# Attention and mixture of experts on one core: softmax sums inverted in two parts, row statistics by two tiles

## The chip, the core and the metric

The kernel runs on one NeuronCore of a Trainium2 chip. Engines are TensorE (PE in the profile, its weight loads PEld), VectorE (DVE), ScalarE (ACT), GpSimd (POOL) and SyncE (SP). Each works through its own queue in order, and they meet in semaphores. The metric is the device time of one execution in microseconds; lower is better.

## The reference, cut to what matters

For 2048 tokens of width 256, with 16 heads:

```python
x = x + layernorm(attention(layernorm(x)))      # causal, latent keys and values of width 64
x = x + layernorm(ffn(layernorm(x)))            # shared expert + 2 of 16 experts per token

scores = einsum('bhqd,bhkd->bhqk', qs, ks_) * scale
attn = softmax(where(causal, scores, min), axis=-1)
out = einsum('bhqk,bhkd->bhqd', attn, v) @ wo
router_logits = x @ gate_w
_, selected = top_k(sigmoid(router_logits) + expert_bias, 2)
```

## The kernel before, in words

The 2048 queries are four blocks of 512 (`qc` 0 to 3), each of four tiles of 128 rows (`TC`). In a block the 16 heads are taken as eight pairs (`p` 0 to 7), and each pair goes over the block's key tiles: 4, 8, 12 or 16 of them, as the attention is causal. One key tile of a pair is three slots, so a pair has 12, 24, 36 or 48 slots.

In a slot, hand-written order: TensorE makes the scores of the pair (`scores`, L1699, with `kt` the key tile and `s` the head), ScalarE the exponentials into a ring of four tiles of probabilities (`scores_to_probs`, L759), GpSimd adds the probabilities up (`add_up`, L560 and L567), TensorE multiplies them by the values (`values`, L1720) into PSUM bank `BK_O`. Before its exponentials, a score bank is seeded with minus the row maximum by ScalarE (`seed`, through the `copy` of L646). The maxima are those of the next pair, made in the same slots one pair ahead: TensorE makes rough scores (`max_unit`, L1673) into banks 4 and 5, VectorE takes their maxima (`maxima`, L1124, L1126), then per head TensorE spreads the maxima over columns (`spread`, L1681) into bank `BK_M` and VectorE copies them out (`widen`, L1142). `units_by` says how many of these units are due at a slot. VectorE also folds each pair's added probabilities into `Lp` (`part_sums`, L1182). Blocks 1 and 2 project the next block's queries in their slots, and block 3 casts the experts' weights (`cut_expert`).

At the end of a block come, by TensorE's order: primes and filler matmuls (`stay_busy`, L1662, which write zeros into a bank that is free), the sums of all 16 heads from `Lp` (L1844), ten fillers, the turning of the inverse sums (L1852), three fillers. VectorE takes the reciprocal (L1360) and splits it into three 16-bit terms (`terms`, L1211 to L1215), ScalarE copies the turned terms out as `inv_rows`. TensorE spreads a pair's inverse sums over its rows (`inv_spread`, L1823), VectorE multiplies the pair's values by them (`normalised`, L1223), and TensorE multiplies by the output weights (`out_product(j, n)`, tile `j`, pair `n`, L1832). Each tile then has its statistics on VectorE, a root on ScalarE, the input added, statistics and root again, and scaled rows (`out_moments`, `with_input`, `row_moments`, `row_scale`, and on ScalarE `root` and `normalised_rows`). VectorE's `choose` and `places` pick the experts of the block before. The next block's first scores wait for the third tile's rows, its first exponential stands on ScalarE behind the fourth tile's last root:

```python
for j in range(TC):
    root(qc, j, 0)
    if 0 < j < TC - 1:
        normalised_rows(qc, j - 1)
    if j < TC - 1:
        root(qc, j, 1)
    if j == TC - 2 and qc < NC - 1:
        act.wait_ge(primed, 2 * (qc + 1) + 2)
        seed(qc + 1, 0, 1)
```

After block 3, the rows are transposed (`turn_xn2`, L1607), routed, and the experts run on gathered rows.

Of the kernel before, what the change touches and what calls it, by code (L numbers as in the profile page):

```python
# [58 lines left out]
ROOTS = 2 + (NT - TC) // 2  # L59

# [15 lines left out]
def attention_moe(nc, x, wq, wkv_a, wkv_b, wo, kv_scale, gate_w, bias, sh_gate, sh_up, sh_down,  # L76
                  ex_gu, ex_down, c32_d, c16_d, out):
    with ExitStack() as ctx:  # L78
# [116 lines left out]
        mask_row = c32[:, C_COS + 2 * CQ:C_COS + 2 * CQ + CQ // 2].bitcast(BF16)  # L195

# [42 lines left out]
        den_read, log_out = sem("den_read"), sem("log_out")  # L239
# [32 lines left out]
        def units_by(slot, qc, p):  # L272

            nq = qc + (p == NP - 1)
            U, slots = units(nq), 3 * tiles_of(qc)
            if Q_IN_LOOP(qc) and p % 2 and nq == qc:

                return min(U, sum(TURN_UNITS[:slot]) + max(slot - len(TURN_UNITS), 0))
            return min(U, slot + min(slot, max(U - slots, 0)))

        def spread_slots(qc, p):
# [5 lines left out]
            second = units(nq) + (4 if Q_IN_LOOP(qc) and p % 2 else 2)  # L287
            return first, min(second, 3 * tiles_of(qc))
# [35 lines left out]
        def inv_bank(n):  # L324

            return BK_O if n % 2 else BK_M

        def first_root(qc, j):

            return ROOTS + 2 * (qc * TC + j)  # L330

# [300 lines left out]
        def _(act):  # L632
# [111 lines left out]
            def scores_to_probs(qc, p):  # L744
# [4 lines left out]
                for kt in range(KT):  # L749
# [42 lines left out]
            def root(qc, j, r):  # L792

                act.wait_ge(var_ready, first_root(qc, j) + r + 1)
                nc.scalar.activation(std[:, TC * r + j:TC * r + j + 1], var[:, TC * r + j:TC * r + j + 1],
                                     ACT.Sqrt).then_inc(std_ready, 1)

            def normalised_rows(qc, j):

                y, x1 = (ysb3, x13) if qc == NC - 1 else (yb, xb)  # L800
                act.wait_ge(scale_ready, qc * TC + j + 1)
# [29 lines left out]
            for qc in range(NC):  # L831
                if qc == NC - 1:
                    act.wait_ge(shared_in, 80)
                    copy(WEh[:, NE, :], stage[:, 0, :], WS).then_inc(raw_hi, 1)
# [4 lines left out]
                if qc:  # L839
                    root(qc - 1, TC - 1, 1)  # L840
# [8 lines left out]

                if qc < NC - 1:  # L850
                    act.wait_ge(primed, 2 * (qc + 1) + 1)
                    seed(qc + 1, 0, 0)

                act.wait_ge(turned_ready, qc + 1)
                copy(inv_rows[0:3 * H, :], ps[0:3 * H, BK_O, :]).then_inc(inv_ready, 1)
                if qc < NC - 1:
                    act.wait_ge(rows_out, 32 * qc)
                for j in range(TC):
# [1157 lines left out]
```

## Time and profile before

| | |
|---|---|
| median of 3 runs | 1311.3 us (1304.27 to 1312.95) |
| the profiled execution | 1306.9 us |
| its span, first to last instruction | 1305.1 us |
| mean granted TensorE clock | 0.968 |
| TensorE busy | 1154.6 us (88%) |
| VectorE busy | 832.9 us (64%) |
| ScalarE busy | 795.2 us (61%) |
| GpSimd busy | 732.5 us (56%) |

In a timeline a row gives the start, the busy time, the engine, the line, what is written and read, and the number of instructions put together; in brackets stands the idle time of the engine before it and what ended that. Times are microseconds from the span's start. A matmul's printed time includes its way through the array, so starts follow one another more closely than these times say.

### The profile page before, as it was taken

What the parts mean: (1) busy time and instruction counts of PE and PEld (TensorE: products, weight loads), DVE (VectorE), ACT (ScalarE), POOL (GpSimd) and SP (SyncE); (2) the same over time, 40 slices, a digit from 0 to 9 for tenths busy, and PEclk for the clock granted to TensorE, in tenths of its full rate; (3) what the DMA queues carried; (4) which work ended last, traced back from release to release, by engine and by line L of the source; (5) the groups of instructions that cost most, each with busy time, mean ns of one, the idle gap of its engine ahead of it and who ended that gap; (6) DMA issues with size and microseconds to landing.
All of it is one profiled execution on the core that took longest, in us unless ns stands there. A gap on an engine that the chain in (4) does not pass through costs nothing. (4 is left out here: it accounts for less than half of the span.)

```text
span 1305.1 us, 19781 instructions
## 1 busy us (share of the span) xinstructions
PE 1154.6 (88%) x6552; PEld 549.4 (42%) x6563; DVE 832.9 (64%) x2104; ACT 795.2 (61%) x1237; POOL 732.5 (56%) x444
## 2 busy tenths in 40 slices
PE   3997999999998999999999979999999999788820
PEld 2643545344443533444443523333433334466710
DVE  6556786666667766565756786676666625745637
ACT  3633762766665466766666367777787783356632
POOL 0046541465564076766666248888888894435545
PEclk9988999999999999999999999999999999989975
DMA  9135300110011010000011001000000000367754
GB/s 286 34 87 131 91 1 1 49 33 17 21 45 34 6 44 17 17 17 17 17 33 32 11 13 57 26 13 13 25 25 25 13 13 17 71 130 211 187 135 141
DMA packets 63031, 70.25 MB, mean 54 GB/s; under 512 B 10080, under 2 KB 52448, under 8 KB 62816
## 3 DMA queue, kind: packets, MB, share of 16 engines
q1 hardware_dynamic: 56656, 56.26, 15.8%
q0 software_dynamic: 4864, 10.51, 3.7%
q10 hardware_dynamic: 1424, 2.38, 0.7%
q8 instruction: 48, 0.79, 0.3%
q14 instruction: 39, 0.32, 0.1%
HBM read 37.51 MB, written 14.83 MB: 40 GB/s over the span
## 5 line engine op out<-in xcount | busy, mean ns | idle before, releaser
L567 POOL TENSOR_TENSOR D<-D,B 128x1024 f32<-128x1024 f32 (+3 forms) x256 | 513.4, 2006 | 140.5 <-ACT B L759 120.2
L759 ACT ACTIVATE B<-ps 128x1024 f32<-128x1024 f32 (+1 forms) x320 | 285.2, 892 | 206.6 <-PE ps L1699 121.0
L1124 DVE TENSOR_REDUCE mxp<-ps 128x1 f32<-128x512 f32 x384 | 260.4, 688 | 177.2 <-PE ps L1673 175.1
L646 ACT ACTIVATE ps<-D 128x1024 f32<-128x1024 f32 (+3 forms) x327 | 288.3, 883 | 24.1 <-DVE D L1142 14.4
L1720 PE MATMUL ps<-B,kv 128*64 128x512 f32 (+3 forms) x1280 | 278.9, 545 | 0.3
L1699 PE MATMUL ps<-A,KTh 128*128 128x512 f16 (+3 forms) x768 | 209.0, 354 | 4.0 <-ACT ps L646 3.9
L560 POOL TENSOR_TENSOR D<-B 128x1024 f32<-128x1024 f32 (+1 forms) x32 | 70.8, 2213 | 209.1 <-ACT B L759 209.1
L1126 DVE CUSTOM_DVE_ANT_0 ps<-ps,c 128x128 f32<-128x128 f32 (+3 forms) x256 | 126.6, 496 | 76.9 <-PE ps L1673 73.4
L1673 PE MATMUL ps<-KTh,A 128*128 128x512 f16 (+3 forms) x384 | 134.4, 357 | 10.4 <-DVE mxp L1124 8.7
L1699 PE MATMUL ps<-A,KTl 128*128 128x512 f16 (+3 forms) x384 | 135.8, 354 | 0.0
L1720 PEld LDWEIGHTS ps<-B,kv 128*64 128x64 f32 x1280 | 73.6, 135 | 113.7 <-issue 97.0
L1699 PEld LDWEIGHTS ps<-A,KTh 128*128 128x128 f16 x768 | 67.6, 98 | 82.0 <-issue 21.4
L1673 PEld LDWEIGHTS ps<-KTh,A 128*128 128x128 f16 x384 | 37.0, 97 | 113.3 <-DVE mxp L1124 45.4
L646 ACT ACTIVATE C<-ps 128x256 f16<-128x256 f32 (+2 forms) x112 | 52.5, 470 | 50.5 <-PE ps L1893 15.5
L586 POOL DMA_INDIRECT B<-xn_rows,tok_i x48 | 45.4, 946 | 50.1 <-PE ps L1893 49.2
L1699 PE MATMUL ps<-WEh,KTh 128*128 128x512 f16 (+3 forms) x256 | 67.1, 345 | 2.5 <-ACT ps L646 2.3
L1832 PE MATMUL ps<-WO,C 128*128 128x256 f32 x256 | 64.7, 393 | 3.1 <-DVE C L1223 3.1
L1699 PE MATMUL ps<-WEl,KTh 128*128 128x512 f16 (+3 forms) x256 | 65.8, 340 | 0.6 <-ACT ps L646 0.6
L1541 PE MATMUL ps<-xnTh,WQh 128*128 128x512 f16 (+1 forms) x160 | 55.5, 347 | 4.5 <-DVE WEl L1260 1.8
L646 ACT ACTIVATE B<-ps 128x256 f32<-128x256 f32 (+2 forms) x132 | 44.0, 336 | 21.9 <-PE ps L1852 17.0
L1701 PE MATMUL ps<-c 128*128 128x128 bf16 x256 | 56.3, 220 | 0.0
L1543 PE MATMUL ps<-xnTh,WQl 128*128 128x512 f16 (+1 forms) x160 | 55.3, 346 | 0.0
(273 smaller groups left out, 1785.3 us busy)
## 6 DMA issues: line engine op xcount, KB each, us to landing
results<-B SPq DMA_DIRECT2D x64, 128.0 KB
xnTl<-in_L_ffn_experts_gate_up SPq DMA_DIRECT2D x16, 256.0 KB, 2.8
A<-in_L_attn_wq SPq DMA_DIRECT2D x4, 768.0 KB, 20.6
B<-in_L_attn_x SPq DMA_DIRECT2D x5, 512.0 KB, 5.6
D<-in_L_attn_wo SPq DMA_DIRECT2D x2, 1024.0 KB, 20.3
A<-C SPq DMA_DIRECT2D x16, 128.0 KB, 2.3
A<-C SPq DMA_DIRECT2D x32, 64.0 KB, 2.0
A<-stg SPq DMA_DIRECT2D x16, 128.0 KB, 2.3
```

The lines of the kernel that those rows point to most:

```text
L560: ins = nc.gpsimd.tensor_tensor(acc[:, :, c0:], Pr[:, 0, :, c0:], Pr[:, 1, :, c0:], ALU.add)
L567: nc.gpsimd.tensor_tensor(acc[:, :, c0:], acc[:, :, c0:], Pr[:, kt % P_RING, :, c0:], ALU.add).then_inc(sum_done, 1)
L646: return nc.scalar.activation(dst, src, ACT.Copy, scale=scale)
L759: nc.scalar.activation(Pr[:, kt % P_RING, :, c0:], ps[:, 2 * (kt % ST_RING):2 * (kt % ST_RING) + 2, c0:], ACT.Exp, scale=SM_SCALE).then_in ...
L1124: V.tensor_reduce(most, rough, AX.X, ALU.max).then_inc(mx_free, 1)
L1126: V.tensor_tensor_reduce(rough, rough, mask_qk(w), 1.0, 2 * NEG, ALU.add, ALU.max, most).then_inc(mx_free, 1)
L1541: T.matmul(dst, ah, bh, start=first, stop=False)
L1673: T.matmul(ps[:, b, 0:w], qt(qc, 2 * p + s, 0)[:, i4 * P:(i4 + 1) * P], KTh[:, kc * CQ:kc * CQ + w], start=True, stop=True).then_inc(mx_re ...
L1699: ins = T.matmul(ps[:, bk, c0:], k[:, keys], v, start=False, stop=True, skip_group_check=True)
L1701: ins = T.matmul(ps[:, bk, c0:c0 + P], identb, mask_kq, start=False, stop=True, skip_group_check=True)
L1720: ins = T.matmul(ps[LORA * s:LORA * (s + 1), BK_O, c0:], kv[:, kt, 0:LORA], Pr[:, kt % P_RING, s, c0:], start=(kt == 0), stop=(kt == KT - 1))
L1832: ins = T.matmul(ps[:, y_bank(j), 0:E], OT[:, o:o + P], WO[:, n, :], start=(n == 0), stop=(n == NP - 1))
```

## The change

The inverse sums of pairs 0 to 5 are made inside pair 7: TensorE makes the sums at one slot and turns the terms at a later one, given for each block in `EARLY`, VectorE makes the reciprocal and its terms in the slot after the first, ScalarE copies the turned terms out. At the block's end only pairs 6 and 7 (`LATE_PAIRS`) are left for the old way, and the fillers there are four instead of 18 (after block 3, 29). The output products of tiles 0 and 1 start at once on pairs 0 to 5. VectorE and ScalarE handle the row statistics of two tiles at a time. The next block's first scores wait for the second tile's rows instead of the third's; the maxima made in pair 0 start four slots later (`HEAD_SLOTS`), and the cast of the shared expert's weights moves from the start of block 3 into its pair 0.

```diff
+EARLY = [(3, 6), (18, 21), (24, 28), (6, 10)]
+LATE_PAIRS = 2
+HEAD_SLOTS = 4
...
+            if qc and p == 0:
+
+                return min(U, max(slot - HEAD_SLOTS, 0))
...
         def inv_bank(n):
 
-            return BK_O if n % 2 else BK_M
+            return 2 + n % 2
...
+                    if qc == NC - 1 and p == 0 and kt == 3:
+                        act.wait_ge(shared_in, 80)
+                        copy(WEh[:, NE, :], stage[:, 0, :], WS).then_inc(raw_hi, 1)
...
+                    if p == NP - 1 and kt == EARLY[qc][1] // 3:
+                        act.wait_ge(e_turned_ready, qc + 1)
+                        copy(early_rows[0:3 * H, :], ps[0:3 * H, BK_M, :]).then_inc(e_inv_ready, 1)
...
-                for j in range(TC):
-                    root(qc, j, 0)
-                    if 0 < j < TC - 1:
-                        normalised_rows(qc, j - 1)
...
+                roots_of(qc, 0, 0)
+                roots_of(qc, 0, 1)
+                roots_of(qc, 2, 0)
+                normalised_rows(qc, 0)
                 if qc < NC - 1:
-                    act.wait_ge(rows_out, 32 * qc)
...
+                    act.wait_ge(primed, 2 * (qc + 1) + 2)
+                    seed(qc + 1, 0, 1)
+                normalised_rows(qc, 1)
+                roots_of(qc, 2, 1)
...
+                    if p == NP - 1 and slot == EARLY[qc][0] + 1:
+                        dve.wait_ge(e_den_ready, qc + 1)
+                        link(V.reciprocal(rL[:, :, :].rearrange("p h j -> p (h j)"), ps[:, BK_M, 0:H * TC]))
+                        terms(early_terms, early_rest, e_terms_ready)
...
+                for n in range(2):
+                    normalised(qc, n)
                 part_sums(qc, NP - 1)
+                for n in range(2, NP - LATE_PAIRS):
+                    normalised(qc, n)
...
+                out_moments(qc, 0)
+                if qc:
+                    places(qc - 1, 1, 3)
+                with_input(qc, 0)
+                row_moments(qc, 0)
+                out_moments(qc, 2)
+                row_scale(qc, 0)
+                with_input(qc, 2)
+                row_moments(qc, 2)
+                row_scale(qc, 2)
...
+                    if p == NP - 1 and slot == EARLY[qc][0]:
+
+                        pe.wait_ge(l_done, CR_L + qc * NP + NP - LATE_PAIRS)
+                        pe.wait_ge(wide_done, 2 * (nq * NP + np_) + int(Q_IN_LOOP(qc)))
+                        sums_of_parts(BK_M, e_den_ready)
+                    if p == NP - 1 and slot == EARLY[qc][1]:
+                        pe.wait_ge(e_terms_ready, qc + 1)
+                        turn_terms(early_terms, BK_M, e_turned_ready)
...
-                stay_busy(5 if qc < NC - 1 else 16)
...
-                stay_busy(10)
...
-                stay_busy(3)
...
+                stay_busy(4, 1)
+                for n in range(NP - LATE_PAIRS):
+                    for j in range(2):
+                        out_product(j, n)
+                    if n + 2 < NP - LATE_PAIRS:
+                        inv_spread(n + 2)
+                    if n == 2:
+
+                        pe.wait_ge(l_done, CR_L + (qc + 1) * NP)
+                        sums_of_parts(0, den_ready)
...
+                pe.wait_ge(terms_ready, qc + 1)
+                turn_terms(inv_terms, 1, turned_ready)
...
+                for j in range(3):
+                    for n in range(NP - LATE_PAIRS, NP):
+                        out_product(j, n)
...
+                for n in range(NP):
+                    out_product(3, n)
                 if qc < NC - 1:
-                    pe.wait_ge(z_ready, qc * TC + 3)
...
+                    pe.wait_ge(z_ready, qc * TC + 2)
```

TensorE in pair 7 of block 1, from slot 18 on, first the order of before, then that of the changed kernel. `KTh` with `WEh` is a unit of the next block's maxima, `KTh`, `KTl` with `A` are scores, `B` with `kv` values, and `Lp` the sums.

```order
L1673 MATMUL ps<-KTh,WEh 128x512
L1699 MATMUL ps<-A,KTh 128x256 x2
L1699 MATMUL ps<-A,KTl 128x256
L1701 MATMUL ps<-c 128x128
L1673 MATMUL ps<-KTh,WEh 128x512
L1720 MATMUL ps<-B,kv 64x512 x2
L1673 MATMUL ps<-KTh,WEh 128x384
L1699 MATMUL ps<-A,KTh 128x128 x2
L1699 MATMUL ps<-A,KTl 128x128
L1701 MATMUL ps<-c 128x128
L1673 MATMUL ps<-KTh,WEh 128x512
```

```order
L1757 MATMUL ps<-Lp,c 32x64 x4
L1702 MATMUL ps<-KTh,WEh 128x512
L1728 MATMUL ps<-A,KTh 128x256 x2
L1728 MATMUL ps<-A,KTl 128x256
L1730 MATMUL ps<-c 128x128
L1702 MATMUL ps<-KTh,WEh 128x512
L1749 MATMUL ps<-B,kv 64x512 x2
L1702 MATMUL ps<-KTh,WEh 128x384
L1728 MATMUL ps<-A,KTh 128x128 x2
L1728 MATMUL ps<-A,KTl 128x128
L1730 MATMUL ps<-c 128x128
L1764 MATMUL ps<-c,scr_r 48x128 x4
```

The sums (L1757) now stand ahead of slot 18's unit, and the turning of the terms (L1764) between the scores of the last key tile's first head and slot 21's unit. VectorE at the same place, before and changed:

```order
L1124 TENSOR_REDUCE mxp<-ps 128x1 x2
L1126 ISA ps,mxp<-ps,c 128x384
L1126 ISA mxp 128x1
L1124 TENSOR_REDUCE mxp<-ps 128x1 x2
L1126 ISA ps,mxp<-ps,c 128x512
```

```order
L1138 TENSOR_REDUCE mxp<-ps 128x1 x2
L1178 RECIPROCAL rL<-ps 128x64
L1233 CAST scr_r<-rL 128x16x4
L1234 TENSOR_TENSOR scr_r<-rL,scr_r 128x64
L1236 CAST scr_r<-scr_r 128x16x4
L1237 TENSOR_TENSOR scr_r<-scr_r 128x16x4
L1140 ISA ps,mxp<-ps,c 128x384
L1140 ISA mxp 128x1
L1138 TENSOR_REDUCE mxp<-ps 128x1 x2
```

The reciprocal and its four terms stand between the units of slots 19 and 20. TensorE at the end of block 1, from the last values product, before and changed; `c` alone is a prime, a filler or (64x512) a spread of inverse sums, `WO,C` an output product:

```order
L1720 MATMUL ps<-B,kv 64x128 x2
L1656 MATMUL ps<-c 128x512 x2
L1662 MATMUL ps<-c 128x512 x5
L1844 MATMUL ps<-Lp,c 32x64 x4
L1662 MATMUL ps<-c 128x512 x10
L1852 MATMUL ps<-c,B 48x128 x4
L1662 MATMUL ps<-c 128x512 x3
L1823 MATMUL ps<-B,c 64x512 x4
L1832 MATMUL ps<-WO,C 128x256
L1823 MATMUL ps<-B,c 64x512 x2
L1832 MATMUL ps<-WO,C 128x256
```

```order
L1749 MATMUL ps<-B,kv 64x128 x2
L1882 MATMUL ps<-c 64x512 x4
L1691 MATMUL ps<-c 128x512 x4
L1891 MATMUL ps<-WO,C 128x256 x2
L1882 MATMUL ps<-c 64x512 x2
L1891 MATMUL ps<-WO,C 128x256 x2
L1882 MATMUL ps<-c 64x512 x2
L1891 MATMUL ps<-WO,C 128x256 x2
L1882 MATMUL ps<-c 64x512 x2
L1757 MATMUL ps<-Lp,c 32x64 x4
L1891 MATMUL ps<-WO,C 128x256 x2
L1882 MATMUL ps<-c 64x512 x2
```

The output products now follow the last values product after two spreads and four fillers, two tiles per pair, and the sums of the late pairs stand behind the third pair's products.

## Rows read from the trace of the kernel before

**Rows 1.** Stretches: start:end, length, busy time (instructions) of PE, PEld, DVE, ACT, POOL; clock, DMA.
```profile
234.40:402.00 167.60, 163.13 (x954) 69.89 (x954) 111.48 (x263) 110.49 (x141) 94.91 (x50) 1.00 0.13 32
...
757.10:760.30 3.20, 3.13 (x9) 1.21 (x10) 1.66 (x5) 2.65 (x4) 0.00 (x0) 0.51 0.38 123
```

**Rows 2.** Timeline of TensorE from the end of block 1 into block 2.
```profile
421.70 0.38 PE L1656 MATMUL ps<-c 128*128 128x512 bf16 x1 [0.16 <-issue]
...
423.49 2.33 PE L1662 MATMUL ps<-c 128*128 128x512 bf16 x10
...
428.74 0.40 PE L1823 MATMUL ps<-B,c 48*64 48x512 bf16 x2
...
439.30 7.07 PE L1832 MATMUL ps<-WO,C 128*128 128x256 f32 x32
446.21 0.59 PE L1699 MATMUL ps<-WEh,KTh 128*128 128x512 f16 x2
...
453.56 0.60 PE L1699 MATMUL ps<-WEh,KTh 128*128 128x512 f16 x2 [0.98 <-ACT ps L646]
```

**Rows 3.** Timeline of ScalarE from the end of block 1 into block 2.
```profile
449.17 0.20 ACT L795 ACTIVATE std<-var 128x1 f32<-128x1 f32 x1 [1.69 <-DVE var L974]
...
450.68 1.02 ACT L759 ACTIVATE B<-ps 128x1024 f32<-128x1024 f32 x1
451.60 0.59 ACT L802 ACTIVATE WEh<-WEl,shiftb,rstd 128x256 f32<-128x256 f32 x1
...
452.49 1.01 ACT L646 ACTIVATE ps<-D 128x1024 f32<-128x1024 f32 x1
```

**Rows 4.** Timeline of TensorE after block 3, the row transposes.
```profile
1118.58 1.09 PE L1607 MATMUL ps<-c,B 128*128 128x128 f32 x8 [0.59 <-ACT B L804]
```

**Rows 5.** Timeline of VectorE at the end of block 1.
```profile
423.69 0.56 DVE L1360 RECIPROCAL rL<-ps 128x64 f32<-128x64 f32 x1 [0.61 <-PE ps L1844]
424.28 0.31 DVE L1211 CAST B<-rL 128x64 bf16<-128x64 f32 x1
...
425.28 0.44 DVE L1215 TENSOR_TENSOR B<-B 128x64 bf16<-128x64 f32 x1
...
439.52 0.42 DVE L1228 BATCH_NORM_STATS2 st<-ps 128x6 f32<-128x256 f32 x1
```

**Rows 6.** Timelines of TensorE and VectorE in pair 7 of blocks 0 to 3.
```profile
195.75 0.39 PE L1673 MATMUL ps<-KTh,A 128*128 128x512 f16 x1
...
417.05 0.38 PE L1673 MATMUL ps<-KTh,WEh 128*128 128x512 f16 x1
...
719.37 1.29 DVE L1124 TENSOR_REDUCE mxp<-ps 128x1 f32<-128x512 f32 x2 [0.23 <-PE ps L1673]
...
720.83 0.38 PE L1673 MATMUL ps<-KTh,A 128*128 128x512 f16 x1
...
1057.14 1.94 PE L1720 MATMUL ps<-B,kv 128*64 128x512 f32 x8
```

**Rows 7.** Timeline of GpSimd in pair 7 of blocks 1, 2 and 3.
```profile
412.33 6.59 POOL L567 TENSOR_TENSOR D<-D,B 128x1024 f32<-128x1024 f32 x4 [3.06 <-ACT B L759]
...
720.25 4.32 POOL L567 TENSOR_TENSOR D<-D,B 128x1024 f32<-128x1024 f32 x2 [1.11 <-ACT B L759]
...
1057.28 32.68 POOL L567 TENSOR_TENSOR D<-D,B 128x1024 f32<-128x1024 f32 x14
```

**Rows 8.** Timelines of GpSimd and VectorE; two VectorE lines, ns min/median/max.
```profile
767.13 2.35 POOL L567 TENSOR_TENSOR D<-D,B 128x1024 f32<-128x1024 f32 x1 [0.51 <-ACT B L759]
...
767.25 2.25 DVE L1331 CAST where_i<-where 128x8 uint32<-128x8 f32 x1
...
L1302 DVE TENSOR_TENSOR share<-share,rsum x4: 166/168/2091, 467.5 to 1187.2; 128x8 f32<-128x8 f32 x4
...
L1321 DVE COPY scr_r<-place x4: 182/183/187, 457.4 to 1127.8; 128x64 f32<-128x64 f32 x4
```

**Rows 9.** Timeline of TensorE in the first pair of block 3.
```profile
757.17 0.61 PE L1673 MATMUL ps<-KTh,A 128*128 128x512 f16 x1 [2.82 <-DVE mxp L1124]
```

More of the change, by code:

```diff
@@ L287, in spread_slots @@
             second = units(nq) + (4 if Q_IN_LOOP(qc) and p % 2 else 2)
+            if qc and p == 0:
+                first, second = first + HEAD_SLOTS, second + HEAD_SLOTS
             return first, min(second, 3 * tiles_of(qc))
@@ new lines, in row_moments, with row_scale @@
+            def row_moments(qc, j0):
+                x1 = x13 if qc == NC - 1 else xb
+                for j in (j0, j0 + 1):
+                    dve.wait_ge(z_ready, qc * TC + j + 1)
+                    ins = V.bn_stats(st6[:, TC + j, :], x1[:, j, :])
+                link(ins)
+                for j in (j0, j0 + 1):
+                    ins = V.bn_aggr(mv[:, TC + j, :], st6[:, TC + j, :])
+                link(ins)
+                variance(TC + j0 + 2, LN_EPS, first=TC + j0)
+            def row_scale(qc, j0):
+                two = slice(TC + j0, TC + j0 + 2)
+                one_over(TC + j0 + 2, first=TC + j0)
+                V.scalar_tensor_tensor(out=shiftb[:, two], in0=mv[:, two, 0], scalar=-1.0, in1=rstd[:, two],
@@ L1722, in values, with sums_of_parts, turn_terms @@
                 ins.then_inc(pv_done, 1)
+            def sums_of_parts(bank, ready):
+                parts = Lp[:, :, :].rearrange("p h (j b) -> p h j b", b=4)
+                for b in range(4):
+                    ins = T.matmul(ps[32 * b:32 * b + 32, bank, 0:H * TC], quads, parts[:, :, :, b],
+                                   start=True, stop=True)
+                ins.then_inc(ready, 1)
+            def turn_terms(terms, bank, ready):
+                for j in range(TC):
+                    ins = T.matmul(ps[0:3 * H, bank, j * P:(j + 1) * P],
+                                   terms[:, j, :, :].rearrange("p w h -> p (w h)"), identb,
+                                   start=True, stop=True)
+                ins.then_inc(ready, 1)
             def pair(qc, p):
@@ L1817, in inv_spread @@
                 def inv_spread(n):
+                    rows = early_rows if n < NP - LATE_PAIRS else inv_rows
                     if n >= 2:
@@ L1847, in _ @@
-                pe.wait_ge(o_free, CR_O + (qc + 1) * NP)
-                stay_busy(10)
-                pe.wait_ge(terms_ready, qc + 1)
-                for j in range(TC):
-                    ins = T.matmul(ps[0:3 * H, BK_O, j * P:(j + 1) * P],
-                                   inv_terms[:, j, :, :].rearrange("p w h -> p (w h)"), identb,
-                                   start=True, stop=True)
-                ins.then_inc(turned_ready, 1)
-                stay_busy(3)
-                pe.wait_ge(inv_ready, qc + 1)
```

171 lines of the change are left out of this document (76 added, 95 removed).

## The prediction

> **What bounds the kernel now.** I read the stretches first. Inside the attention blocks TensorE is the pace: it is busy 163.1 of 167.6 us at the full clock in block 1 [rows 1]. Between the blocks it isn't. TensorE's timeline of the end of block 1 [rows 2] shows 24.5 us from the last values product (421.70) to the next block's first scores (446.21), of which 18 filler matmuls (5, 10 and 3 by the code; the ten take 2.33) do nothing, and the inverse sums go through VectorE, TensorE and ScalarE before the first output product can start. ScalarE's timeline [rows 3] shows what comes last there: the root of the fourth tile's second variance (449.17), the table load behind it, and only then the next block's first exponential (450.68), 29.0 us after 421.70. TensorE takes up scores again 2.9 us after that exponential (453.56), once the next seed is in. The same distance is 28.8 and 28.9 us after blocks 0 and 2; block 3 has no next block and ends in the row transposes at 1118.58 [rows 4]. So the change has to be judged by three things: what it puts into the full last pairs, how much earlier the next exponential comes, and how much earlier the transposes come.
>
> **Term A, the early sums inside the last pair.** Each block's pair 7 gets four more sums matmuls and four turning matmuls on TensorE (about 0.35 us each group, 0.7 together), one copy of 0.6 us on ScalarE, and on VectorE a reciprocal, two casts and two subtractions, which took 2.03 us in a row from 423.69 to 425.72 [rows 5]. TensorE now waits in its own queue for those terms before it turns them, so scores, maxima and values behind it stand. What counts is when VectorE gets to the reciprocal and when the terms are done.
>
> Where TensorE comes to the turning is read from the matmul that follows it now [rows 6]: 195.75 in block 0, 417.05 in block 1, 720.83 in block 2, 1057.14 in block 3. VectorE has to do the maximum ahead of the reciprocal first. In block 2 that is the first of the two from 719.37 [rows 6], which the sums put off by 0.35, so it ends at 720.4; by the same reading it ends at 195.6 and 416.7 in blocks 0 and 1. In block 3 it has no maxima, so the sums, done at about 1054.8, start it. With 2.0 us for the terms and 0.35 for turning, the matmul behind comes 2.3, 2.1 and 2.1 us late in blocks 0 to 2 (198.1, 419.2, 722.9), and not late in block 3, where the terms would be done at 1056.9. Nothing gives that back: TensorE has no idle time behind it in block 2, and in blocks 0 and 1 its one wait there is for VectorE's maxima, which come later by the same step.
>
> But GpSimd adds up probabilities just then [rows 7], and small VectorE operations between SBUF tiles are held by it: the cast of 0.17 us took 2.25 us from 767.25 and ended with the GpSimd addition that had begun at 767.13, and a subtraction-like operation of 0.17 us took 2.09 [rows 8]. I take the two subtractions as held and the two casts as free, because these casts (0.31 us, 16-bit results written with a stride) don't run at the speed of the plain copy of as many elements (0.18 us) [rows 5, 8]. Block 0: an addition ends at 197.4, the next needs an exponential that TensorE now keeps back; terms at 198.5, turned at 198.85, 3.1 us late. Block 1: the third of the four additions ends at about 418.35 (the sums themselves shift it by 0.35); terms at 419.45, 2.8 late. Block 2: two additions follow each other, ending at 722.6 and 724.5; the first subtraction waits for one, the second for the other; terms at 725.0, 4.6 late. Block 3: additions end at 1057.14 and 1059.7, terms at 1060.15, turned at 1060.5. There GpSimd is what bounds the pair, 14 additions without a pause to 1089.96 [rows 7]; its fifth addition comes 2.9 us later than now (values 1.9, scores 1.3, exponential 1.0 behind 1060.5, against 1057.28 and two additions of 2.33, 1061.95). Sum of A: 3.1 + 2.8 + 4.6 + 2.9 = 13.4. Bounds: all terms free, 2.3 + 2.1 + 2.1 + 0 = 6.5; casts held too, one more addition in blocks 2 and 3, 3.6 + 3.0 + 5.2 + 5.5 = 17.3.
>
> The Trainium skill's page SBUF — State Buffer, section Who interferes with whom, says that a VectorE instruction with two SBUF inputs, or a copy or cast in a two-port mode, and a GpSimd instruction shut each other out for the whole instruction. The held rows agree with it. By it alone the casts would be held where they run in that mode, which makes A 17.3 and is the slower rival below; if it did not bite here, A would be 6.5.
>
> **Term B, the stretch between blocks.** Worked out on block 1. TensorE from 421.70: two spread pairs (0.33 us each), four fillers (0.9); then per pair two output products (0.87, as 32 passes take 7.07) and a spread, 1.2 us against VectorE's 0.7, so TensorE no longer waits for VectorE; sums, turning, primes. Together 64 passes 14.1 + eight spreads 2.7 + 0.9 + 0.75 + 0.9 = 19.3: it is through at 441.0, 5.2 earlier. VectorE's terms (done 431.2) and ScalarE's copy lie beside products of tiles 0 to 2.
> The next exponential gains less. Tiles 0 and 1 are complete at 436.2; two statistics (0.42 each, [rows 5]), aggregates and variance to 437.2; table load and root to 438.75; scale and two multiply-adds to 439.95; second statistics to 441.25. Tiles 2 and 3 follow: variance 442.45, multiply-adds 443.9, second variance 445.25. ScalarE in the meantime does row pair 0, seed and row pair 1 (0.89, 1.0 and 0.89 by [rows 3]) from 442.8 to 445.6; root to exponential takes 1.51, so the exponential is at 447.1 instead of 450.68: 3.6 earlier. This takes the place of the single-tile chain; last is now ScalarE's row pair 1, 0.3 behind VectorE. Three blocks: 10.8.
> Block 3: the last part sum needs GpSimd's end at 1090; the sixth pair's products end at 1096.5, terms 1097.6 and VectorE's choice of experts to 1099.3, late pairs' products to 1103.0, tile 3 to 1106.7. Then second variance 1110.75 and two row pairs to 1113.3, against 1118.5: 5.2 earlier, and all that follows moves with it. B = -(10.8 + 5.2) = -16.0. Bounds: TensorE's own gain between the blocks, -(3 x 5.2 + 5.2) = -20.8; each ScalarE and VectorE operation at its full printed time instead of the distance of starts, -(3 x 2.7 + 4.0) = -12.1.
>
> **Terms C and D.** C: the maxima of pair 0 start four slots later. TensorE has then done two instead of six of them when it takes up scores again, 0.86 us of work moved into a full stretch, less its waits for VectorE there (up to 1.0 a block); 0.4 per block, 1.2, bounds 0 and 2.6. The shared weights' cast (0.83 us ScalarE, 0.95 VectorE) moves off the start of block 3, but that start waits for the root chain anyway: nothing; it would cost its own 0.95 once if VectorE's maxima in pair 0 waited on it.
> D: the clock. TensorE stood idle for 2.82 us before 757.17 [rows 9], and the 3.2 us from 757.10 ran at a granted clock of 0.51, the 1.2 GHz level [rows 1]; the wait of 0.98 before 453.56 was followed by full-speed matmuls [rows 2]. One such loss is 1.5 us. In the changed kernel TensorE has nothing from about 446.6 to 449.95 (3.4 us) after block 1, and as much after block 0; block 3's start had its loss already. The stop in block 2's last pair is 3.8 us. So three losses, 4.5; bounds 0 and five (with block 3's stop and the wait before the transposes), 7.5.
>
> **Sum.** 13.4 - 16.0 + 1.2 + 4.5 = +3.1. The profiled execution took 1306.9 us (span 1305.1), 4.4 below the median of 1311.3 of the runs shown, so 1310.0 beside it and 1314.4, rounded 1314, beside the median. About 1% (13 us) is what a measurement of this kernel can tell from no change.
>
> **Rivals.** First, faster: VectorE's early terms meet GpSimd idle or aren't held, and the stop in block 2 costs no clock. Then 6.5 - 16.0 + 1.2 + 3.0 = -5.3, 1306. For it: every row of the same five operations ran free [rows 5]; against: those ran while GpSimd was idle. Second, faster by more: TensorE's own 5.2 us decide between the blocks, not the exponential, and no clock is lost: 6.5 - 20.8 + 0 + 0 = -14.3, 1297. Against it stands the 2.9 us between exponential and scores, which only ScalarE sets. Third, slower: GpSimd holds all four early operations, and each long stop loses the clock: 17.3 - 16.0 + 1.2 + 7.5 = +10.0, 1321; in block 3, at half clock, values and scores behind the stop take 3.2 us more and GpSimd's row of additions ends later by as much, 1324.5. It decides from the point where terms take longer than 4 us instead of 2.0; the held cast speaks for it [rows 8]. Fourth, the change doesn't do what it says: the exponential waits as now for the last tile's root, the three 3.6 us are not gained: +13.9, 1325.
>
> **Chances and range.** Forecast 0.43, first rival 0.27, second 0.12, third 0.14, fourth 0.04. The range 1300 to 1324 leaves out the second rival and the upper half of the third and fourth, about 0.2. Faster by over 1% (below 1298): the second rival and a bit, 0.13; slower by over 1% (above 1324): 0.13; within 1%: 0.74.
>
> **What would show it.** Term A: in the last pairs VectorE's four early operations should take over 1 us more than 1.5 in blocks 2 and 3, with TensorE idle for 2 to 5 us ahead of its turning matmuls. If these are free everywhere, A is wrong and the time is at most 1306. Term B: first exponential 25.4 us after the last values product instead of 29.0, transposes 23.3 us after GpSimd's last addition instead of 28.6. Term D: granted clock near 0.5 for some 3 us at the start of blocks 1 and 2. A time outside 1300 to 1324 would make the whole wrong.

## The result and the profile after

| | before | changed |
|---|---|---|
| median of the runs | 1309.37 us (4 runs, 1304.27 to 1312.95) | 1324.06 us (4 runs, 1321.1 to 1325.84) |
| ratio to before | | 1.0113, 95% interval 1.0071 to 1.0154 |
| profiled execution, span | 1305.1 us | 1323.0 us |

The change makes the kernel 14.7 us slower where 3.1 more were forecast; 1324.06 lies just outside the range of 1300 to 1324.

Where the 17.9 us between the two profiles lie is read best from ScalarE's exponentials, 320 in both, always in the same order. Each stretch runs between the starts of two of them: of a last pair from its first to its last, of a first pair, and of pairs 1 to 6, from its first to the first of the pair behind. The last column is the prediction's terms, put at the stretch they were meant for.

| stretch, by ScalarE's exponentials | before | changed | difference | predicted |
|---|---|---|---|---|
| start of the program to pair 1 of block 0 | 139.83 | 141.26 | +1.4 | 0 |
| block 0, pairs 1 to 6 | 50.94 | 50.94 | 0 | 0 |
| block 0, pair 7, first to last | 8.06 | 14.10 | +6.0 | 3.1 |
| last of block 0 to first of block 1 | 32.69 | 29.26 | -3.4 | -3.6 |
| block 1, pair 0 | 20.96 | 22.81 | +1.9 | 0.4 + 1.5 |
| block 1, pairs 1 to 6 | 141.28 | 141.28 | 0 | 0 |
| block 1, pair 7 | 23.93 | 26.64 | +2.7 | 2.8 |
| last of block 1 to first of block 2 | 32.99 | 29.35 | -3.6 | -3.6 |
| block 2, pair 0 | 33.51 | 35.74 | +2.2 | 0.4 + 1.5 |
| block 2, pairs 1 to 6 | 206.60 | 206.61 | 0 | 0 |
| block 2, pair 7 | 34.29 | 42.22 | +7.9 | 4.6 + 1.5 |
| last of block 2 to first of block 3 | 31.84 | 28.47 | -3.4 | -3.6 |
| block 3, pair 0 | 46.62 | 51.83 | +5.2 | 0.4 |
| block 3, pairs 1 to 6 | 248.06 | 248.05 | 0 | 0 |
| block 3, pair 7, to GpSimd's last addition | 38.37 | 45.21 | +6.8 | 2.9 |
| from there to the row transposes | 28.61 | 23.37 | -5.2 | -5.2 |
| behind the row transposes | 186.53 | 185.82 | -0.7 | 0 |

Between the blocks the prediction holds within 0.3 us everywhere. The last pairs cost 23.5 us instead of 14.9, the first pairs of blocks 1 to 3 cost 9.3 instead of 4.2. These are the two errors, 8.6 and 5.1 us.

**The gain between the blocks, as forecast.** TensorE's timeline of the changed kernel from the end of block 1 into block 2, which answers to [rows 2]:

```profile
429.84 0.62 PE L1882 MATMUL ps<-c 48*64 48x512 bf16 x4
...
437.08 2.86 PE L1891 MATMUL ps<-WO,C 128*128 128x256 f32 x12
...
449.75 0.59 PE L1728 MATMUL ps<-WEh,KTh 128*128 128x512 f16 x2
...
454.78 0.59 PE L1702 MATMUL ps<-KTh,WEh 128*128 128x512 f16 x2
458.51 1.04 PE L1728 MATMUL ps<-WEh,KTh 128*128 128x512 f16 x2 [3.14 <-ACT ps L661]
```

ScalarE's timeline of the same place, which answers to [rows 3]:

```profile
446.06 1.28 ACT L817 ACT_TABLE_LOAD   x1 [2.56 <-DVE var L988]
...
453.25 0.58 ACT L823 ACTIVATE WEh<-WEl,shiftb,rstd 128x256 f32<-128x256 f32 x1
...
455.63 1.02 ACT L774 ACTIVATE B<-ps 128x1024 f32<-128x1024 f32 x1
```

Products start as soon as the last values product is through (429.84), scores of block 2 are issued 19.9 us behind it instead of 24.5, and the first exponential stands 25.8 us behind it (455.63) instead of 29.0. Then TensorE has nothing to do for 3.14 us: the stop is nearly as long as the prediction had it (3.4). The row transposes come 23.4 us behind the end of GpSimd's last addition (1113.77), against 28.6 [rows 4, 7]. GpSimd's and TensorE's timelines:

```profile
1086.09 27.68 POOL L582 TENSOR_TENSOR D<-D,B 128x1024 f32<-128x1024 f32 x12 [7.01 <-ACT B L774]
...
1137.14 1.40 PE L1636 MATMUL ps<-c,B 128*128 128x128 f32 x8 [2.38 <-ACT B L825]
```

**The stops in the last pairs.** VectorE's timeline of the early sums in block 2, where [rows 5] has the same five operations with GpSimd idle:

```profile
727.64 0.55 DVE L1178 RECIPROCAL rL<-ps 128x64 f32<-128x64 f32 x1
728.22 2.20 DVE L1233 CAST scr_r<-rL 128x64 bf16<-128x64 f32 x1
730.46 1.86 DVE L1234 TENSOR_TENSOR scr_r<-rL,scr_r 128x64 f32<-128x64 f32 x1
732.36 0.31 DVE L1236 CAST scr_r<-scr_r 128x64 bf16<-128x64 f32 x1
732.70 0.44 DVE L1237 TENSOR_TENSOR scr_r<-scr_r 128x64 bf16<-128x64 f32 x1
```

GpSimd's timeline there: two additions, from 727.91 to 732.20.

```profile
727.91 4.29 POOL L582 TENSOR_TENSOR D<-D,B 128x1024 f32<-128x1024 f32 x2 [1.55 <-ACT B L774]
```

The cast of 0.31 us took 2.20: it waited for the first of the two additions, the subtraction behind it for the second, and ended 0.12 us after it (732.32 against 732.20). The groups of these operations by line, over all four blocks (busy us, mean ns of one). The reciprocal, which reads PSUM, has its usual length, and the last subtraction, which met no addition in any block, has its own:

```profile
L1233 DVE CAST scr_r<-rL 128x64 bf16<-128x64 f32 x4 | 5.8, 1456 | 0.1
L1234 DVE TENSOR_TENSOR scr_r<-rL,scr_r 128x64 f32<-128x64 f32 x4 | 4.9, 1216 | 0.1
L1236 DVE CAST scr_r<-scr_r 128x64 bf16<-128x64 f32 x4 | 3.4, 856 | 0.1
...
L1178 DVE RECIPROCAL rL<-ps 128x64 f32<-128x64 f32 x4 | 2.2, 551 | 8.2 <-PE ps L1757 8.2
...
L1237 DVE TENSOR_TENSOR scr_r<-scr_r 128x64 bf16<-128x64 f32 x4 | 1.8, 445 | 0.1
```

TensorE's stops at the turning, in blocks 0 to 3:

```profile
200.28 0.62 PE L1764 MATMUL ps<-c,scr_r 128*48 128x128 bf16 x4 [2.87 <-DVE scr_r L1237]
...
425.30 0.40 PE L1764 MATMUL ps<-c,scr_r 128*48 128x128 bf16 x4 [1.74 <-DVE scr_r L1237]
...
733.20 0.62 PE L1764 MATMUL ps<-c,scr_r 128*48 128x128 bf16 x4 [4.54 <-DVE scr_r L1237]
...
1079.78 0.51 PE L1764 MATMUL ps<-c,scr_r 128*48 128x128 bf16 x3 [5.61 <-DVE scr_r L1237]
```

Three of the four turnings take 0.5 or 0.6 us instead of 0.40: behind these stops the clock is down. The stretches (columns as in [rows 1]; the clock is the third figure from the end) show block 1 at full clock and then the slow ones: behind the stops of blocks 0, 2 and 3, at the start of block 2, and two in the first pair of block 3:

```profile
238.40:418.00 179.60, 172.97 (x1004) 74.27 (x1005) 121.63 (x286) 115.76 (x147) 99.65 (x52) 1.00 0.13 32
200.20:206.20 6.00, 5.92 (x29) 2.87 (x29) 2.72 (x10) 1.07 (x2) 1.27 (x1) 0.52 0.00 1
458.50:461.90 3.40, 3.39 (x9) 1.30 (x10) 2.47 (x4) 3.40 (x6) 1.84 (x1) 0.50 0.26 58
733.20:738.70 5.50, 5.50 (x18) 1.72 (x19) 1.74 (x5) 0.59 (x1) 0.00 (x0) 0.53 0.00 0
772.50:775.90 3.40, 3.35 (x10) 0.85 (x9) 3.20 (x7) 3.37 (x5) 2.98 (x2) 0.51 0.00 0
787.00:793.10 6.10, 6.03 (x14) 1.61 (x15) 3.53 (x9) 0.00 (x0) 1.61 (x1) 0.51 0.18 64
1079.80:1083.40 3.60, 3.60 (x12) 1.39 (x12) 0.00 (x0) 0.59 (x1) 0.00 (x0) 0.53 0.00 0
```

The stop at the start of block 1 is about as long as that of block 2 (3.14), and the clock stays up behind it:

```profile
238.44 0.60 PE L1728 MATMUL ps<-A,KTh 128*128 128x512 f16 x2 [3.30 <-ACT ps L661]
```

**The shared cast in the first pair of block 3.** VectorE's timeline of the kernel before, then VectorE's, GpSimd's and TensorE's of the changed kernel:

```profile
755.29 0.95 DVE L1347 SCALAR_TENSOR_TENSOR WEl<-xnTl,WEh 128x768 f16<-128x768 f32 x1
```

```profile
783.48 2.93 DVE L1195 SCALAR_TENSOR_TENSOR WEl<-xnTl,WEh 128x768 f16<-128x768 f32 x1
```

```profile
783.25 2.34 POOL L582 TENSOR_TENSOR D<-D,B 128x1024 f32<-128x1024 f32 x1 [2.85 <-ACT B L774]
785.75 2.86 POOL L582 TENSOR_TENSOR D<-D,B 128x1024 f32<-128x1024 f32 x1 [0.15 <-ACT B L774]
```

```profile
787.07 0.61 PE L1702 MATMUL ps<-KTh,A 128*128 128x512 f16 x1 [2.46 <-DVE mxp L1138]
787.61 3.68 PE L1749 MATMUL ps<-B,kv 128*64 128x512 f32 x8
```

The cast had taken 0.95 us at the start of block 3. Moved between GpSimd's additions it takes 2.93, the maxima behind it come late, TensorE stops for 2.46 us, and the eight values products behind the stop take 3.68 us instead of 1.94.

### The profile page after: what moved, and what is told of

Read it like the earlier page. It is cut to its first block and busy times, and to the rows that moved or that the text cites. A ratio compares the mean times of both kernels' runs of the same rounds, so it can differ in the third digit from the quotient of the medians.

```text
span 1323.0 us, 19712 instructions
## 1 busy us (share of the span) xinstructions
PE 1147.7 (87%) x6533; PEld 547.6 (41%) x6544; DVE 841.4 (64%) x2077; ACT 793.6 (60%) x1225; POOL 736.2 (56%) x444
## 5 line engine op out<-in xcount | busy, mean ns | idle before, releaser
L1749 PE MATMUL ps<-B,kv 128*64 128x512 f32 (+3 forms) x1280 | 285.0, 554 | 0.3
L589 POOL TENSOR_TENSOR B<-B 128x512 f32<-128x512 f32 x5 | 6.3, 1265 | 88.2 <-DVE B L1105 88.2
```

What stands on the lines that cost most here:

```text
L1749: ins = T.matmul(ps[LORA * s:LORA * (s + 1), BK_O, c0:], kv[:, kt, 0:LORA], Pr[:, kt % P_RING, s, c0:], start=(kt == 0), stop=(kt == KT - 1))
```

## The experiments

The theory after this reading: GpSimd's additions hold every VectorE operation that works from SBUF to SBUF, casts too; TensorE stops for them in the last pairs and in block 3's first pair, and its clock falls behind the stops. The rivals: TensorE's own place in its queue (too few slots between sums and turning), and the later start of the first maxima.

The ratios below are to runs of the kernel before that were taken beside each group of versions, with a median of 1313.07 us for the first five and of 1309.96 us for the four that put things together; so versions are compared by ratio and not by time. Fillers and the two profiles taken once more are single runs (1327.46, 1319.45 and 1329.11 us), read by their stretches alone.

The growth of each stretch against the kernel before, in us, from one profile of each version (first pairs of blocks 1 to 3; last pairs of blocks 0 to 3, the last to GpSimd's last addition; the three stretches between blocks; from GpSimd's last addition to the transposes):

| version | first pairs | last pairs | between blocks | to transposes |
|---|---|---|---|---|
| the change | 1.9, 2.2, 5.2 | 6.0, 2.7, 7.9, 6.8 | -3.4, -3.6, -3.4 | -5.2 |
| the change, second profile | 1.9, 2.2, 5.3 | 5.0, 2.7, 8.1, 6.9 | -3.4, -3.6, -3.4 | -5.2 |
| shared cast back | 3.5, 2.2, 1.3 | 3.4, 2.7, 8.1, 7.2 | -3.3, -3.6, -3.4 | -5.2 |
| terms through PSUM | 3.5, 2.2, 2.4 | 2.9, 2.5, 2.4, 0.0 | -3.3, -3.7, -3.4 | -3.8 |
| wide gap | 1.9, 3.5, 5.1 | 6.3, 3.0, 1.6, 0.0 | -3.4, -3.3, -2.4 | -2.1 |
| maxima from slot 0 | 0.0, 0.0, 3.3 | 6.2, 2.7, 8.0, 7.8 | -3.4, +0.5, -3.4 | -5.2 |
| fillers in block 3's stop | 3.5, 2.2, 5.4 | 3.4, 2.7, 8.1, 5.2 | -3.3, -3.7, -3.4 | -5.3 |
| PSUM, cast back | 3.5, 2.2, 1.1 | 2.9, 2.5, 2.4, 0.0 | -3.3, -3.6, -3.4 | -3.7 |
| PSUM, cast back, wide gap, maxima from slot 0 | 0.0, 0.0, 0.4 | 4.3, 2.5, 1.8, 0.0 | -3.4, -3.3, -2.4 | -3.8 |
| PSUM, cast back, maxima from slot 0 | 0.0, 0.0, 0.4 | 4.4, 2.5, 2.4, 0.0 | -3.3, -3.6, -3.4 | -5.2 |

**Shared cast back.** ScalarE's part between two roots of block 2's tail, VectorE's part ahead of block 3's first maxima:

```diff
-                    if qc == NC - 1 and p == 0 and kt == 3:
-                        act.wait_ge(shared_in, 80)
-                        copy(WEh[:, NE, :], stage[:, 0, :], WS).then_inc(raw_hi, 1)
...
                 roots_of(qc, 0, 0)
+                if qc == NC - 2:
+                    act.wait_ge(shared_in, 80)
+                    copy(WEh[:, NE, :], stage[:, 0, :], WS).then_inc(raw_hi, 1)
                 roots_of(qc, 0, 1)
...
-                    if qc == NC - 1 and p == 0 and slot == 13:
-                        dve.wait_ge(raw_hi, 1)
...
             for qc in range(NC):
+                if qc == NC - 1:
+                    dve.wait_ge(raw_hi, 1)
...
                 for p in range(NP):
```

> The shared expert's cast goes back out of block 3's first pair: ScalarE's part between the two roots of block 2's tail, VectorE's part ahead of block 3's first maxima, where GpSimd has nothing to do. Theory: in the first pair of block 3 the VectorE part was held by GpSimd's additions (2.93 us instead of 0.95), the maxima behind it came late, TensorE stopped for 2.46 us and then ran at half clock. Then the growth of that pair (5.2 us against the kernel before) falls below 1.5 and the whole comes to about 1319.5 us. Rival: the four slots by which the maxima start later are the cause; then the growth stays at 4 to 5 us and the time at 1324.

Measured: 1322.22 us, ratio 1.0079 (1.0049 to 1.011). The first pair of block 3 grows by 1.3 us instead of 5.2. VectorE's part, with GpSimd idle:

```profile
771.42 0.95 DVE L1373 SCALAR_TENSOR_TENSOR WEl<-xnTl,WEh 128x768 f16<-128x768 f32 x1
```

The theory holds for this pair: 4.0 us are the held cast, its stop and its clock; 1.3 are left, of which the later maxima are a part. Of the whole time the intervals of the two versions overlap, so the 4 us are shown by the profile alone.

**Terms through PSUM.** The reciprocal writes into free columns of the bank it reads, the remainder stays there too; nothing else moves:

```diff
-link(V.reciprocal(rL[:, :, :].rearrange("p h j -> p (h j)"), ps[:, BK_M, 0:H * TC]))
-terms(early_terms, early_rest, e_terms_ready)
+link(V.reciprocal(ps[:, BK_M, H * TC:2 * H * TC], ps[:, BK_M, 0:H * TC]))
+terms(early_terms, ps[:, BK_M, 2 * H * TC:3 * H * TC].rearrange("p (h j) -> p h j", h=H),
+      e_terms_ready, ps[:, BK_M, H * TC:2 * H * TC].rearrange("p (h j) -> p h j", h=H))
...
```

> The early reciprocal and the remainder are kept in PSUM, so each of VectorE's early casts and subtractions reads at least one operand from PSUM; count and order of the instructions stay. Theory: GpSimd's additions hold VectorE only where all its operands are in SBUF. Then the four operations take 1.5 to 2 us in every last pair (in the changed kernel 2.1, 1.9, 4.9 and 7.2), the growth of the four last pairs (6.0, 2.7, 7.9 and 7.5, together 24.2 us) falls to some 8 to 10, and the time is about 1309. Rival: they are slow because of the 16-bit results written with a stride into SBUF beside GpSimd's own writes; then they stay as long and the time stays at 1324.

Measured: 1313.7 us, ratio 1.0014 (0.9988 to 1.004). The groups by line, to be laid beside those of the change:

```profile
L1234 DVE CAST scr_r<-ps 128x64 bf16<-128x64 f32 x4 | 1.8, 445 | 0.1
L1237 DVE CAST scr_r<-ps 128x64 bf16<-128x64 f32 x4 | 1.8, 444 | 0.1
L1238 DVE TENSOR_TENSOR scr_r<-ps,scr_r 128x64 bf16<-128x64 f32 x4 | 1.8, 443 | 0.1
L1235 DVE TENSOR_TENSOR ps<-ps,scr_r 128x64 f32<-128x64 f32 x4 | 1.1, 268 | 0.1
```

In block 3, VectorE and GpSimd now run side by side:

```profile
1061.36 0.45 DVE L1234 CAST scr_r<-ps 128x64 bf16<-128x64 f32 x1
1061.84 0.27 DVE L1235 TENSOR_TENSOR ps<-ps,scr_r 128x64 f32<-128x64 f32 x1
1062.15 0.45 DVE L1237 CAST scr_r<-ps 128x64 bf16<-128x64 f32 x1
1062.63 0.45 DVE L1238 TENSOR_TENSOR scr_r<-ps,scr_r 128x64 bf16<-128x64 f32 x1
```

```profile
1060.59 2.35 POOL L575 TENSOR_TENSOR D<-B 128x1024 f32<-128x1024 f32 x1 [0.49 <-ACT B L774]
```

This is the decisive run. Same operations, same slots, same 16-bit results with a stride; what changed is that each reads one operand from PSUM (and the remainder is written there). None of the sixteen is held: the casts take 0.44 to 0.45 us in every block, the subtractions 0.27 and 0.44 as they do with GpSimd idle. The last pairs of blocks 2 and 3 lose 5.5 and 6.8 us of their growth and the kernel some 13 of its 14.7 us (ratio 1.0014 against 1.0113).

The Trainium skill's page SBUF — State Buffer, section Who interferes with whom, names an exclusion between VectorE and GpSimd for two SBUF inputs and for copies and casts in a two-port mode; both kinds were held here and both are free from PSUM. The trace agrees with it on the subtractions; it shows these casts held too, though no run shows whether they ran in such a mode.

These 13 us are not the early terms' alone, because the first pair of block 3 grows by 2.4 us here instead of 5.2. The shared cast is still held there for 2.92 us and TensorE stops for the same 2.46 us behind it, but this time its clock stays at 1.00. VectorE's cast, and TensorE's stretch behind the stop, which answers to the change's 787.00:793.10:

```profile
775.12 2.92 DVE L1196 SCALAR_TENSOR_TENSOR WEl<-xnTl,WEh 128x768 f16<-128x768 f32 x1
```

```profile
778.70:784.80 6.10, 6.09 (x27) 2.10 (x27) 5.76 (x14) 1.93 (x2) 2.42 (x2) 1.00 0.21 64
```

So of the 4.0 us that the shared cast cost in the change, 2.9 were the clock behind its stop. Why the clock stayed up in this profile is not shown.

**Wide gap.** One line:

```diff
-EARLY = [(3, 6), (18, 21), (24, 28), (6, 10)]
+EARLY = [(2, 8), (16, 23), (22, 35), (6, 30)]
```

> The slots alone change: sums at 2, 16, 22 and 6, turning at 8, 23, 35 and 30 of the last pairs instead of 3 and 6, 18 and 21, 24 and 28, 6 and 10. Theory, by the prediction's own step: TensorE's wait for the terms in its own queue is the cost; with the turning this late it is gone in all blocks, the last pairs grow by 1 us each, and the time is about 1303. Rival: VectorE is the one that is late, since the next block's maxima stand behind the held terms; then block 3, which has no maxima, loses its whole growth of 7.5 us, but block 2 still stops for 2 us or more at its maxima, and the time is 1310 to 1314.

Measured: 1317.57 us, ratio 1.0037 (1.0009 to 1.0065). Neither side is right throughout. Blocks 2 and 3 lose 6.4 and 6.8 us, block 2 far more than the rival allowed; blocks 0 and 1 lose nothing (6.3 and 3.0). There TensorE now stops for the next block's maxima, which stand on VectorE behind its terms: 1.53 us in block 1, and in block 0, where the first cast is held for 1.94 us, 3.50:

```profile
199.44 0.61 PE L1702 MATMUL ps<-KTh,A 128*128 128x512 f16 x1 [3.50 <-DVE mxp L1138]
```

In block 2 the run doesn't tell the two sides apart. At their new slot the four terms met hardly any addition (0.39, 0.27, 0.31 and 0.44 us), so the hold went together with the wait. Block 3 does tell them apart: its terms are held longer than in the change (1.75, 2.43, 2.51 and 2.60 us) and cost nothing, as TensorE has other work until slot 30. What costs is thus both together, a held operation and a queue that waits for it. The gap also costs between the blocks: -2.4 instead of -3.4 behind block 2.

**Maxima from slot 0.** `HEAD_SLOTS = 0` instead of 4.

> The first maxima of blocks 1 to 3 start at slot 0 again instead of slot 4. Theory, by the prediction's terms: the late start costs 0.4 us a block and the stop at the block's start remains, so the first pairs' growth (1.9, 2.2 and 5.2 us in blocks 1, 2 and 3) falls by under 1 us each and the time is 1322 to 1324. Rival: the late maxima cause that growth; then it falls to near nothing in blocks 1 and 2, by 4 us in block 3, and the time is about 1316.

Measured: 1324.66 us, ratio 1.0079 (1.0039 to 1.0119). The first pairs of blocks 1 and 2 take exactly their old time again (20.96 and 33.52 us), block 3's loses 2.0. So the rival was right about these pairs and the prediction's term was too small. TensorE's timeline at the start of block 1 shows why:

```profile
233.81 0.39 PE L1702 MATMUL ps<-KTh,A 128*128 128x512 f16 x1 [1.73 <-DVE mxp L1138]
...
236.95 0.60 PE L1728 MATMUL ps<-A,KTh 128*128 128x512 f16 x2 [0.97 <-ACT ps L661]
```

With the early start TensorE does scores and maxima until 236 and then waits 0.97 us for the first exponential's seed; with the late start it waits 3.30 us there, and the maxima come later in a stretch that has no room for them. The whole time doesn't show the gain clear of noise: the five runs lie between 1317.15 and 1327.21 us, and the interval overlaps that of the change. In the profiled one (1324.66 us) the end of block 1 ran at half clock, 10 us long and at the cost of 4 (the +0.5 in the table); whether it did so in the others is not known:

```profile
423.70:433.70 10.00, 8.52 (x32) 3.70 (x30) 5.69 (x10) 2.24 (x4) 0.43 (x1) 0.51 0.00 0
```

**Fillers in block 3's stop.** Only there a bank is free that nobody reads:

```diff
                     if p == NP - 1 and slot == EARLY[qc][1]:
+                        if qc == NC - 1:
+                            pe.wait_ge(mx_free, CR_MX + first_unit(NC))
+                            stay_busy(23, BK_X)
                         pe.wait_ge(e_terms_ready, qc + 1)
```

> In block 3's last pair 23 filler matmuls of zeros (some 0.22 us each, 5.0 together) run into a bank of the maxima, which are over, while TensorE waits the 5.6 us for the held terms. Theory: of that pair's growth of 7.5 us the idle stop itself is one part and the reduced clock behind it another: eight values products took 3.36 us instead of 1.94, 1.4 more. With TensorE busy through the stop these run at full speed and the growth is 6.1. Rival: GpSimd's row of additions hides the slower products; then the growth stays at 7.5.

Measured: growth of the pair to its last exponential 5.9 us instead of 7.5. TensorE's timeline with fillers, and that of the change at the same place:

```profile
1072.41 4.91 PE L1691 MATMUL ps<-c 128*128 128x512 bf16 x22
1077.99 0.35 PE L1764 MATMUL ps<-c,scr_r 128*48 128x128 bf16 x3 [0.67 <-DVE scr_r L1237]
...
1078.23 1.88 PE L1749 MATMUL ps<-B,kv 128*64 128x512 f32 x7
```

```profile
1080.19 3.36 PE L1749 MATMUL ps<-B,kv 128*64 128x512 f32 x7
```

The held terms are as long as before; only the seven products behind the stop run at full speed, 1.88 us against 3.36. So 1.6 us of block 3's growth were the clock, and 5.2 (to GpSimd's last addition) the hold.

**The kernel before and the change, profiled once more.**

> The kernel before, unchanged, profiled a second time. In the first profile 186.5 us lie between the row transposes after block 3 and the end; the profiles with the early sums have 185.8 to 191.8 there. Theory: that spread is the chip's own from one execution to the next (the first exponential, ahead of all edits, comes between 129.0 and 135.8 us in them), so this profile differs from the first by 1 us or more ahead of block 0 or behind the transposes, and agrees with it within 0.2 us in the pairs between. Rival: the transposes' gain is given back behind them; then it shows 186.5 again.

Measured: every stretch between block 0's pair 1 and the transposes agrees within 0.13 us with the first profile, most within 0.01; ahead of block 0 it is 6.5 us longer, and behind the transposes 192.7 instead of 186.5 us. So nothing that the profiles show there (185.8 to 192.7) can be put down to a version, and it is not shown that the 5.2 us of the transposes are given back.

> The changed kernel, unchanged, profiled a second time. Theory: the stops of TensorE in the four last pairs stand where they stood, with the growth of blocks 1, 2 and 3 within 0.5 us of 2.7, 7.9 and 7.5; what TensorE's reduced clock adds moves: block 0's last pair grows by 3.4 us or by 6.0, and the first pair of block 1 by 3.5 or by 1.9, as the reduced clock falls into the one or the other. Rival: the stops themselves vary, and the growth of blocks 2 and 3 is another by over 1 us.

Measured: 2.70, 8.05 and 7.53 us in the last pairs of blocks 1, 2 and 3. Block 0's grew by 5.0, neither of the two values expected: the reduced clock began later. The stops are the change's own; the clock's share in block 0 is not fixed.

**Together.** Four versions, to see what of the change can be kept.

> Early terms through PSUM and the shared cast back in block 2's tail, both at once. Theory: two separate holds by GpSimd, so the gains add: first pair of block 3 grows by about 1.3 us instead of 5.2, the last pairs by 2.9, 2.5, 2.4 and 0.4, and the ratio to the kernel before is 1.0014 less 0.0034, 0.998. Rival: the hold of the cast only moves to the next VectorE operation of that pair once the cast is gone; then the ratio stays at 1.001.

Measured: 1310.48 us, ratio 0.999 (0.9971 to 1.0009). In the profile the gains add: the last pairs stay as they were with the terms through PSUM, and block 3's first pair grows by 1.1 us instead of 2.4. It gains 1.2 us and not 4.0, since the clock there had not fallen with the terms through PSUM alone. In the whole time the two versions' intervals overlap.

> As the one before, with the turning at slots 8, 23, 35 and 30 (sums at 2, 16, 22 and 6). Theory: what is left of the last pairs' growth is TensorE's wait for free-running terms (2.36, 1.49 and 1.33 us ahead of the turning with the terms in PSUM); with the wide gap it falls to some 1 us a block, and the ratio is 0.994. Rival: VectorE sets the pace of the last pairs of blocks 0 to 2, whose maxima wait behind the 2 us of the terms; then the growth stays at 2 to 2.5 us and the ratio at 0.998.

Measured: 1311.75 us, ratio 1.0009 (0.9991 to 1.0027). That is neither 0.994 nor the rival's 0.998. There is no gain over the version without the gap (0.999), which is the rival's side.

> As the one before, and the first maxima of blocks 1 to 3 again from slot 0. Theory: the late start costs 1.9 and 2.2 us in the first pairs of blocks 1 and 2 and about 1 in block 3, also where TensorE's clock is not reduced; then the ratio is 0.004 below that of the version with the late start. Rival: with the early start TensorE stops for the maxima's ring instead and the two are equal.

Measured: 1305.48 us, ratio 0.9967 (0.9947 to 0.9987); 0.0042 below the version with the late start, as expected, and the two intervals don't touch. Where the fastest version below stops for 2.36, 1.49 and 1.34 us at the turning in the last pairs of blocks 0 to 2, this one stops for 2.07, 0.96 and 1.33 us at the maxima that stand behind VectorE's terms. What the gap gains in block 2 (1.8 instead of 2.4) it loses behind it (-2.4 instead of -3.4).

> Early terms through PSUM, the shared cast in block 2's tail, first maxima from slot 0, and the slots of sums and turning as in the change. Theory: 0.004 below the version with the late start, 0.994; and if the wide gap gains nothing, equal to the version with both. Rival: the late start costs nothing once the other two are gone, 0.998.

Measured: 1304.7 us over 12 runs against 1309.96, ratio 0.9953 (0.9931 to 0.9975). This has the lowest ratio, though its interval overlaps that of the version with the gap. It keeps the change's early sums and tails, and undoes what it gave away. What is left in its last pairs (2.5 and 2.4 us in blocks 1 and 2; 4.4 in block 0 with a slow stretch) is probably VectorE's 2.2 us of reciprocal and terms, for which TensorE waits at one place or another; no run takes them away.

## Why the prediction failed, step by step

- **What bounds the kernel now: right.** The three places by which the change was to be judged changed, and besides them only the first pairs of terms C and D; pairs 1 to 6 agree within 0.01 us.
- **Term B: right in mechanism and size.** -3.4, -3.6, -3.4 and -5.2 against three times -3.6 and -5.2: -15.7 in place of -16.0. ScalarE's row pairs and the table load were indeed last.
- **Term A: wrong at one step**, "I take the two subtractions as held and the two casts as free, because these casts don't run at the speed of the plain copy". The casts were held: 1.03, 0.83, 2.20 and 1.76 us for the first, 2.49 for the second in block 3, all against 0.31. That a cast alone is slower than a copy says nothing of whether GpSimd holds it. The four last pairs without the clock come to 3.4 (shared cast back, block 0), 2.7, about 5.3 (an estimate: 7.9 less what the clock cost in block 0) and 5.2 (fillers): 16.6, beside the upper bound of 17.3 that was worked out for held casts, where 13.4 was taken. With the terms through PSUM, so without any hold, the four come to 7.8 against the 6.5 of the prediction; the hold itself is thus some 8.8, against 6.9. Block 3 is where the held casts show: three additions waited for, and not two. Block 1's 2.8 came out with another split (2.5 of its 2.7 stay without the hold), which is luck.
- **Term D: mis-sized and partly misplaced.** Three losses of 1.5 were taken. In the last pairs the clock fell behind three of four stops, at 2.87, 4.54 and 5.61 us of idling; it cost 2.6 in block 0 (6.0 against 3.4 without it) and 1.6 in block 3 (with and without fillers), and with the estimate for block 2 some 6.9 in all where 1.5 was taken. This is the largest part of the miss in the last pairs. In block 3's first pair it fell once more than before and cost 2.9. At the start of block 1 it cost nothing in the profile of the change, whose stretch stands at 1.00; in other profiles it fell there and cost 1.6 (3.5 against 1.9). The size of one short loss was right; how many, and how long, was not.
- **Term C: mis-sized.** 0.4 a block was taken with a bound of 2.6 for all three; with the early start restored the pairs lost 1.9, 2.2 and 2.0, block 2's slow stretch included (block 3's with the shared cast still in it). The maxima had been filling TensorE's wait for the first exponential. The prediction saw the work move ("0.86 us of work moved into a full stretch") but set against it TensorE's waits for VectorE, which didn't shrink: in block 2's first pair those for the maxima are 1.44 us before and 1.43 after. In block 1 C and D together came to the right 1.9, for the wrong reason.
- **The shared cast: wrong.** "nothing; it would cost its own 0.95 once if VectorE's maxima in pair 0 waited on it." It cost 4.0: some 1.1 by the hold, as TensorE stops for 2.46 us there and for 1.25 with the cast back, and 2.9 by the clock behind that stop. The row of the held cast in that very pair [rows 8] was used for the terms, and not for the other operation moved there.
- **The sum.** 23.5 (last pairs with their clock) + 9.3 (first pairs) - 15.7 = 17.1 us in the profile from block 0's pair 1 to the transposes, against 14.9 + 4.2 - 16.0 = 3.1. Of the 14.0 us between them, about 5.4 are clock lost behind the stops of the last pairs, 2.9 the clock behind the shared cast's stop, and 3.2 term A. The other 2.5 are the hold of the shared cast, the later maxima and 0.3 of term B. So the casts taken as free are the step that was argued wrongly, and what the stops did to the clock, which term D had too small, is the larger price.
- **The rivals.** The third, all four early operations held and the stops losing clock, is what happened; its sum of +10.0 (or 13.2 with block 3's clock) missed mainly the shared cast. It was given 0.14. Its point of decision (terms over 4 us instead of 2.0) was met in blocks 2 and 3 (4.9 and 7.2 us from the first cast to the last subtraction). That its 1324.5 stands so near the measured 1324.06 is luck, as the shared cast is not in it.

## What to carry to other kernels

Before moving small VectorE operations into a stretch where GpSimd streams, list for each whether all its operands are in SBUF; those that are can wait for the end of the GpSimd instruction they meet, and a queue that waits for them stops for as long. Where a PSUM bank is at hand, let the chain read from it: that took away the hold at 0.13 us per cast. Work that fills an engine's wait is not free to be moved: ask what the engine does in that wait afterwards, and count what the stop leaves behind at the lower clock.

## What the runs showed of the hardware that was not expected

- In the change every held term ended 0.12 to 0.18 us after a GpSimd addition's end (732.32 behind 732.20 in block 2; in block 3 1074.29, 1076.72 and 1079.25 behind 1074.11, 1076.60 and 1079.08). In such a row of additions without a pause one VectorE operation got through per gap, so three operations of 0.3 us took the time of three additions.
- The longer shared cast got through a gap too, and the addition behind that gap took 2.86 us where the one ahead took 2.34: GpSimd seems to be held by VectorE in its turn.
- The same cast takes 0.44 us from PSUM and 0.31 from SBUF; beside GpSimd the slower form is the faster one.
- One stop can cost the granted clock for longer than the stop itself: 2.87 us of idling in block 0 were followed by 6.0 us at 0.52, the 1.2 GHz level. The stop of 3.30 us at the start of block 1 was followed by full speed in both profiles of the change and by the lower level in others (shared cast back, terms through PSUM), with the same instructions around it.
